# Dilated attention: three row loads at the start, a product moved ahead of the first scores, two score banks, and another layout for the queries in DRAM

## The reference, cut to what matters

```python
x = x + jnp.tanh(g_xattn[1]) * _L1_xattn_ref(_layernorm(x, axis=-1), ctx_1024, ctx_1024, ...)
# _L1_xattn_ref: q = x Wq + bq, k and v from the context, 16 heads of 16; per branch (segment, dilation):
scores = jnp.einsum("bqhd,bkhd->bhqk", qd, kd) * D ** (-0.5)
scores = jnp.where(mask, scores, -jnp.inf)
lse = jax.nn.logsumexp(scores, axis=-1)
o = jnp.einsum("bhqk,bkhd->bqhd", jnp.exp(scores - lse[..., None]), vd)
```

## Time and profile before

| | us |
|---|---|
| median of 3 runs | 838.92 (836.3 to 841.04) |
| the profiled execution, its own time | 843.52 |
| its span, first to last instruction | 841.8 |
| PE busy in the span | 638.2 (76%) |
| DVE busy | 503.8 (60%) |
| ACT busy | 429.2 (51%) |
| POOL busy | 352.3 (42%) |
| mean granted clock of PE, of full speed | 0.866 |

### The profile page before, as it was taken

How to read it: one execution, slowest core, us unless ns; L and a number is a source line. 1 busy time by engine, 2 the same in 40 slices (tenths; PEclk the granted TensorE clock), 3 DMA queues, 4 the chain that set the end, 5 groups by cost and what they waited for, 6 DMA issues and landing times. The chain is left out here.

```text
span 841.8 us, 14246 instructions
## 1 busy us (share of the span) xinstructions
PE 638.2 (76%) x4856; PEld 477.8 (57%) x4856; DVE 503.8 (60%) x1627; ACT 429.2 (51%) x815; POOL 352.3 (42%) x482
## 2 busy tenths in 40 slices
PE   3989899649999999999524778877987732138995
PEld 2878778427778778877412445544544521026774
DVE  0466655866666666664115577778775617857741
ACT  1353532218766876677111466556755616417753
POOL 2133325273563365353312443444533316534644
PEclk9998999859999999999855798889988955559998
DMA  6244214263553465342311222223210015503433
GB/s 194 69 124 140 85 51 143 97 190 91 137 152 95 104 142 151 93 87 32 49 52 32 59 77 63 81 57 97 81 39 28 26 38 189 194 26 73 85 52 38
DMA packets 73881, 76.07 MB, mean 90 GB/s; under 512 B 8037, under 2 KB 66449, under 8 KB 73553
## 3 DMA queue, kind: packets, MB, share of 16 engines
q1 hardware_dynamic: 61217, 59.32, 22.2%
q0 software_dynamic: 10928, 15.57, 11.0%
q10 hardware_dynamic: 1664, 0.27, 0.2%
HBM read 52.20 MB, written 22.94 MB: 89 GB/s over the span
## 5 line engine op out<-in xcount | busy, mean ns | idle before, releaser
L1876 DVE CUSTOM_DVE_ANT_0 c_sn<-c_ps_s,k_mask 128x128 f32<-128x128 f32 (+1 forms) x256 | 75.8, 352 | 55.3 <-PE c_ps_s L2014 55.3
L1708 POOL TENSOR_SCALAR_AFFINE_SELECT c_pr<-c_pr 128x512 f32<-128x512 f32 x64 | 42.9, 671 | 108.9 <-ACT c_pr L1767 107.8
L1398 PE MATMUL b_ps_y<-e_w2h,b_hh 128*128 128x256 f16 x320 | 87.3, 273 | 1.4 <-DVE b_yb L1312 0.6
L1398 PE MATMUL b_ps_y<-e_w2l,b_hh 128*128 128x256 f16 x320 | 87.2, 273 | 0.0
L1398 PE MATMUL b_ps_y<-e_w2h,b_hl 128*128 128x256 f16 x320 | 87.2, 273 | 0.0
L1281 DVE TENSOR_TENSOR b_hl<-b_h,b_hh 128x640 f16<-128x640 f32 x64 | 53.2, 832 | 47.5 <-ACT b_hh L1229 47.5
L1207 POOL DMA_INDIRECT res<-b_y,b_s_idx x40 | 65.2, 1631 | 37.7 <-ACT b_y L1246 27.4
L1193 POOL DMA_INDIRECT e_xg<-rows,e_g_idx x35 | 38.6, 1104 | 81.8 <-DVE e_g_idx L1322 71.2
L2042 PE MATMUL c_ps_v<-c_pr,k_vx 128*64 128x256 f32 (+1 forms) x512 | 62.1, 368 | 5.6 <-POOL c_pr L1708 4.8
L1767 ACT ACTIVATE c_pr<-c_ps_t 128x768 f32<-128x768 f32 x64 | 51.7, 808 | 13.2 <-PE c_ps_t L2028 13.2
L1361 PE MATMUL b_ps_h<-b_xh,e_w1h 128*128 128x320 f16 x256 | 56.7, 303 | 1.0 <-DVE b_xl L1286 0.9
(11 more groups left out here) (421 smaller groups left out, 1817.3 us busy)
## 6 DMA issues: line engine op xcount, KB each, us to landing
e_w<-in_L_ffn_W_dram SPq DMA_DIRECT2D x16, 1024.0 KB, 6.0
d_raw<-in_L_ffn_W_down_dram SPq DMA_DIRECT2D x8, 640.0 KB
k_ks<-kT SPq DMA_DIRECT2D x48, 64.0 KB, 2.6
c_qs<-q SPq DMA_DIRECT2D x48, 64.0 KB, 2.4
d_raw<-in_L_ffn_W_up_dram SPq DMA_DIRECT2D x4, 682.0 KB, 4.0
rows<-a_rows SPq DMA_DIRECT2D x8, 264.0 KB, 2.5
rows<-c_rows SPq DMA_DIRECT2D x8, 264.0 KB, 2.2
a_x_in<-in_x_dram SPq DMA_DIRECT2D x8, 256.0 KB, 3.0
```

What stands on the lines that cost most here:

```text
L1398: last = pe.matmul(ps_y[(j + CT) % 2][:, 0:D], a, b[:, f, :], start=(f == 0 and k == 0), stop=(f == FC - 1 and k == 2))
L1708: pool.affine_select(out=late, in_=late, compare_op=ALU.is_ge, fill=0.0, base=0, pattern=[[0, 2], [0, 2], [1, P]], channel_multiplier=-1). ...
L1876: dve.tensor_tensor_reduce(sn[r][:, a:b], ps_s[:, r, a:b], mask[:, a:b], -1.0, 3.0e38, ALU.add, ALU.min, mx[g % 2][:, q, r, j:j + 1]).then ...
```

## The change

What it does, part by part:

- `load_x(0)`, `load_x(1)` and `load_x(2)` are issued together at the start of the stage; the later loads keep their places.
- For batch 1 the turn of xn and the query product (`rows_turn`, `queries`) stand at place 0 of step -2, before batch 0's first score tile, in place of 6 and 7; DVE's `stats` of batch 1 moves to place 0 of that step, behind ql of batch 0.
- Batch 0's score tiles alternate between ps_s and ps_t, each waits for the maxima of the last but one, and sn has four buffers.
- For batch 0 the turn of the maxima stands ahead of batch 1's first score tile, and its first by_keys (with its exp) one place earlier.
- For all batches the queries' way through DRAM is another: `dram["q"]` holds 32 rows of 8 pairs by 256. Each half is stored as soon as it is there, in two DMAs, one for each c; two loads bring the high half into 32 rows each (the same 16 rows twice, a repeat of 2 in front of the source), two more the low half into 16 rows each. There are semaphores for the high and the low store apart.

```diff
-        sn = some(2, "sn", [P, QK])
+        sn = some(4, "sn", [P, QK])
...
+        def first_scores_in_t(g, j):
+            return g == 0 and j % 2 == 1
...
-            load_x(0)
+            for first in range(3):
+                load_x(first)
...
                 if within(f):
-                    landed(sp, s_ldq, f, 2, 96)
+                    landed(sp, s_ldq, f, 2, 64)
                     apart(sp, s_passs)
-                    after(sp, s_qh, f)
-                    after(sp, s_ql, f)
-                    for part, src in enumerate((qh, ql)):
-                        sp.dma_start(dram["q"][f % 2, part].rearrange("(c p) t -> p c t", p=P), src[f % 2][:])\
-                            .then_inc(s_qst[f % 2], 16)
-                    landed(sp, s_qst, f, 0, 32)
+                    for done_, stored, part, src in ((s_qh, s_qsh, 0, qh), (s_ql, s_qsl, 1, ql)):
+                        after(sp, done_, f)
+                        for c in range(C):
+                            sp.dma_start(dram["q"][f % 2, part, :, 4 * c:4 * c + 4, :].rearrange("k b t -> b k t"),
+                                         src[f % 2][:, c, :]).then_inc(stored[f % 2], 16)
+                    landed(sp, s_qsh, f, 0, 32)
                     done(sp, s_pt, (f - 2) * HH)
-                    for part, which in enumerate((0, 0, 1)):
-                        for r in range(2):
-                            a = 64 * r + HD * part
-                            sp.dma_start(qs[f % 3][a:a + HD, :, :], by_head(dram["q"][f % 2, which], HD)[r])\
-                                .then_inc(s_ldq[f % 3], 16)
+                    for r in range(2):
+                        sp.dma_start(qs[f % 3][64 * r:64 * r + 2 * HD, :, :],
+                                     dram["q"][f % 2, 0, r * HD:(r + 1) * HD, :, :].unsqueeze(0)
+                                     .to_broadcast([2, HD, HH, T]))\
+                            .then_inc(s_ldq[f % 3], 16)
+                    landed(sp, s_qsl, f, 0, 32)
+                    for r in range(2):
+                        a = 64 * r + 2 * HD
+                        sp.dma_start(qs[f % 3][a:a + HD, :, :], dram["q"][f % 2, 1, r * HD:(r + 1) * HD, :, :])\
+                            .then_inc(s_ldq[f % 3], 16)
...
-                if within(e + 1):
+                if within(e + 1) and e + 1 >= 3:
                     load_x(e + 1)
...
-                    if p + 1 == HH and within(g):
+                    if p + (2 if g == 0 else 1) == HH and within(g):
                         exps(g, 0)
...
+                bank = ps_t if first_scores_in_t(g, j) else ps_s
...
-                        dve.tensor_tensor_reduce(sn[r][:, a:b], ps_s[:, r, a:b], mask[:, a:b], -1.0, 3.0e38,
+                        dve.tensor_tensor_reduce(sn[2 * (j % 2) + r][:, a:b], bank[:, r, a:b], mask[:, a:b], -1.0, 3.0e38,
...
-                    if p == 4 and within(e):
+                    if p == (0 if e == 1 else 4) and within(e):
                         landed(dve, s_ldx, e)
...
-                done(pe, s_mx, (g * HH + j) * 4)
+                done(pe, s_mx, (j - 1 if g == 0 else g * HH + j) * 4)
+                bank = ps_t if first_scores_in_t(g, j) else ps_s
...
+                    if p == 0 and e == 1:
+                        rows_turn(e)
+                        queries(e)
...
-                    if p + 1 == HH and within(g):
+                    if p + (2 if g == 0 else 1) == HH and within(g):
                         by_keys(g, 0)
                     if p < 4 and within(g):
                         scores(g, p + 4)
+                    if p == 4 and g == 0:
+                        maxima_turn(n, g)
                     if p >= 4 and within(f):
                         scores(f, p - 4)
...
+                    if p == 4 and within(g) and g > 0:
+                        maxima_turn(n, g)
...
-                    if p == 6 and within(e):
...
+                    if p == 6 and within(e) and e != 1:
+                        rows_turn(e)
+                    if p == 7 and within(e) and e != 1:
+                        queries(e)
...
-        "q": nc.dram_tensor("q", [2, 2, S.D, S.T], F16).ap(),
+        "q": nc.dram_tensor("q", [2, 2, 2 * S.HD, S.H // 2, S.T], F16).ap(),
```

More of the change, by code:

```diff
@@ L1572, in attention_dilated @@
         s_ldm = [sem("ldm0"), sem("ldm1"), sem("ldm2")]
-        s_qst = [sem("qst0"), sem("qst1")]; s_mst = [sem("mst0"), sem("mst1")]
+        s_qsh = [sem("qsh0"), sem("qsh1")]; s_qsl = [sem("qsl0"), sem("qsl1")]
+        s_mst = [sem("mst0"), sem("mst1")]
         s_st = sem("st"); s_mv = sem("mv"); s_var = sem("var"); s_rstd = sem("rstd"); s_mr = sem("mr")
@@ L1687, in _ @@
             for u in range(2):
-                for pair, per in ((s_qst, 32), (s_mst, 16), (s_xst, 16), (s_rst, 16)):
+                for pair, per in ((s_qsh, 32), (s_qsl, 32), (s_mst, 16), (s_xst, 16), (s_rst, 16)):
                     sp.wait_ge(pair[u], per * B // 2)
@@ L1842, in step @@
                         after(act, s_qf, e)
-                        landed(act, s_qst, e, 2, 32)
+                        landed(act, s_qsh, e, 2, 32)
                         act.activation(qh[e % 2][:], qf[:], ACT.Copy).then_inc(s_qh, 1)
@@ L1903, in step @@
                         after(dve, s_qh, f)
-                        landed(dve, s_qst, f, 2, 32)
+                        landed(dve, s_qsl, f, 2, 32)
                         dve.tensor_tensor(ql[f % 2][:], qf[:], qh[f % 2][:], ALU.subtract).then_inc(s_ql, 1)
@@ L2013, in scores @@
                         a = 64 * r
-                        last = pe.matmul(ps_s[:, r, lo:hi], q[a:a + 3 * HD, j, rows_], key[a:a + 3 * HD, j, 0:keys],
+                        last = pe.matmul(bank[:, r, lo:hi], q[a:a + 3 * HD, j, rows_], key[a:a + 3 * HD, j, 0:keys],
                                          start=True, stop=True)
@@ L2055, in turned, with maxima_turn, rows_turn, queries @@
                 last.then_inc(s_ot, 1)
+            def maxima_turn(n, g):
+                after(pe, s_mlo, g)
+                done(pe, s_av, n * HH + 4)
+                for q in range(2):
+                    last = pe.matmul(ps_v[0:4 * HH, T + (1 - q) * P:T + (2 - q) * P],
+                                     mhl[g % 2][:, q, :, :, :].rearrange("p r l b -> p (r l b)"), ident_h[:],
+                                     start=True, stop=True)
+                last.then_inc(s_pm, 1)
+            def rows_turn(e):
+                after(pe, s_xn, e, 0, 2)
+                after(pe, s_oT, e, 4)
+                if e:
+                    after(pe, s_xT, e - 1)
+                turn(ps_a, xn[e % 2], swap=True).then_inc(s_pxt, 1)
+            def queries(e):
+                after(pe, s_xT, e)
+                after(pe, s_x3, e, 4, 2)
+                if e:
+                    after(pe, s_qf, e - 1)
+                product(ps_b, wT[:, 0], xT).then_inc(s_pq, 1)
             over_tensor(pe)
@@ L2067, in step @@
                         scores(g, p + 4)
+                    if p == 4 and g == 0:
+                        maxima_turn(n, g)
                     if p >= 4 and within(f):
                         scores(f, p - 4)
-                    if p == 4 and within(g):
-                        after(pe, s_mlo, g)
-                        done(pe, s_av, n * HH + p)
-                        for q in range(2):
-                            last = pe.matmul(ps_v[0:4 * HH, T + (1 - q) * P:T + (2 - q) * P],
-                                             mhl[g % 2][:, q, :, :, :].rearrange("p r l b -> p (r l b)"), ident_h[:],
-                                             start=True, stop=True)
-                        last.then_inc(s_pm, 1)
+                    if p == 4 and within(g) and g > 0:
+                        maxima_turn(n, g)
                     if within(n):
@@ L2107, in step @@
                         product(ps_b, oT, wT[:, 1]).then_inc(s_po, 1)
-                    if p == 6 and within(e):
-                        after(pe, s_xn, e, 0, 2)
-                        after(pe, s_oT, e, 4)
-                        turn(ps_a, xn[e % 2], swap=True).then_inc(s_pxt, 1)
-                    if p == 7 and within(e):
-                        after(pe, s_xT, e)
-                        after(pe, s_x3, e, 4, 2)
-                        product(ps_b, wT[:, 0], xT).then_inc(s_pq, 1)
+                    if p == 6 and within(e) and e != 1:
+                        rows_turn(e)
+                    if p == 7 and within(e) and e != 1:
+                        queries(e)
             for n in range(-3, B + 2):
```

2 lines of the change are left out of this document (1 added, 1 removed).

## The result

The changed kernel took 851.15 us (median of 4 runs, 850.62 to 852.04) against 839.98 for the kernel before on the same chip: a ratio on record of 1.011 with a 95% interval of 1.0069 to 1.0152 (the two medians alone would make it 1.013). The forecast was 839.1 with a range up to 844.0. The time went the way of the third rival (847.7: the two-engine loads set the loop), and the sign that the prediction named for it, a wait for q before every batch, is there.

A forecast was written before the change was run, and what follows sets the result against it. VectorE and TensorE set the loop's length; the start is a filling pipeline with waits for queries. Batch 2's scores 0.15 us earlier plus 0.3 for a colder start gave about +0.2 on 838.92: 839.1, range 833.0 to 844.0.

The forecast's parts named there:

- the third rival: Dilated attention loop: at 0.22 us a 4 KB packet, two-engine high loads delay every batch, 8.8 us slower, 847.7; chance 0.12.
- Shape sets the number of engines: Queries' DRAM transfers: the smaller leading count decides, so new stores run on 4 engines, high loads on 2, low loads on 16.
- Both loads on the same pair, 0.16 us a packet: High-half query loads: both use the same two engines, 32 packets of 4 KB on each, at 0.161 us a packet.
- Stores on four engines: Query stores to DRAM: 512-byte packets at 0.0274 us on 4 engines, 1.75 us for two stores, 3.5 for all four.
- 10.33 us from qh to the scores: Queries through DRAM, from qh's end to first scores: 0.96 + 3.5 + 5.15 + 0.32 + 0.4 us; before, 7.69.
- 32 x 0.161 = 5.15: Time in us of the two high loads: 32 packets of 4 KB on each of two shared engines.
- The margin: Loop, batches 3 to 7: the queries' way could take 1.35 us more than its forecast 10.33 us without cost.
- the point of 11.68 us: Loop: length of the way from qh to the scores up to which it costs nothing; 0.20 us a 4 KB packet.
- Batch 0 behind the second product: Start of dilated attention: batch 0's scores wait for batch 1's product, ending 443.65, 2.68 us later; q(0) lands by 443.61.
- Two banks, 1.12 us a head; ql(1) 4 us earlier: Batch 0's heads run at VectorE's pace, 1.12 us each, so batch 1's low query half ends 4.02 us earlier.
- The reordering loses nothing else: Start of dilated attention: four sn buffers cost nothing; the third x load was taken as 0 for x(0), at most 1.8 us.
- 0.3 for a colder start: Batch 2's scores: 0.3 us added because TensorE waits 4 us for q in place of 1.77.

## Why the prediction was wrong, point by point

- **Shape sets the number of engines**: right, from the closers: 4 a store and 2 a high load came, on 4.4 and 2.03 engines by the share. The runs with four loads (16 closers a load) and with high and low in one (2) show it too.
- **Both loads on the same pair, 0.16 us a packet**: right (2.03 engines; 24 packets of 4 KB in 2 us, and two chains in the packet records).
- **Stores on four engines**: right (16 closers), 0.0273 us a packet (forecast 0.0274).
- **10.33 us from qh to the scores**: wrong, and the step that failed: 12.27 in batch 0, 12.04 to 12.89 in the loop. The term mis-sized is "32 x 0.161 = 5.15" and the 0.32 behind it: 5.47 taken, 6.98 measured in batch 0 and 6.5 to 7.4 in the others. It counted packets at the price of a long quiet run and let both engines start at once. In batch 0 one engine starts 1.38 us late, behind an instruction fetch. In the loop both start within 0.5 us of each other, but their first packets take up to 1.1 us, and the value rows and the low loads pass beside them. Another 0.3 to 0.7 us came ahead of the loads, where 4.46 had been taken.
- **The margin**: the point of 11.68 us was right (11.75 by the ring). With only 1.35 us of margin, and under it a load that no row had shown at work, the third rival deserved more than its 0.12. That rival's way was 12.3 us and its places were nearly these (forecast 23.5, measured 23.44 for batch 0; 8.8 us in all, measured 9.2 by the ratio). Its reason, every packet dearer at 0.22, was not the one: most packets still took 0.16, so the near hit of its sum is partly luck.
- **Batch 0 behind the second product**: right but for q: the product ends 21.39 after the layer norm (forecast 21.53), then TensorE waits 2.04 for q. With a quick q it is 21.33.
- **Two banks, 1.12 us a head; ql(1) 4 us earlier**: right (1.11; 4.25 earlier with the old way of q, 2.3 in the changed kernel, whose scores began late).
- **The reordering loses nothing else**: right; 0.994 alone. The third row load costs nothing, as taken.
- **0.3 for a colder start**: it came (batch 2's first score tile takes 0.50 us at 483.03, at a granted clock of 0.50, where the kernel before has 0.34 at 1.00), but beside a wait of 5.78 us for q it has no weight.

So the gain of the reordering, 5 us, was there. The new way of q, put in to make it larger, took 14 us: part at the start, part in each turn of the loop.

## What to carry to other kernels

Merging two loads of 16 rows into one of 32 by a leading repeat of 2 saves a DMA and gave up 14 of 16 engines here (2 closers a load in place of 16); look at the leading count of both sides, and read it from the closing packets. Where two engines carry a load, its packets stand in two chains, and the load is done with the later one: in batch 0 that was the chain which began 1.38 us late, and it ended 0.51 us after the other. Don't price such a load from a long run on all engines. And where a stall has a slack in a loop, work out the ring (here 15.3 us from scores to qh, and the way back) before trusting a margin of one microsecond.

## What the runs showed of the hardware

- The DMAs followed here leave one packet of 4 bytes (0.009 us) for each engine that carries them. With two: in the changed kernel's batch 0 each of the two chains has one at the end of each high load, and the share there is 2.03 engines. With four: 16 for four stores led by 4, at 4.4 engines. With sixteen: 32 for two stores led by 128, at 14.6 engines, in the kernel before.
- Some of the first packets of a load on two engines are long. In the changed kernel's dilated attention the trace's packet records hold 16 packets of 4 KB that took 0.6 to 1.1 us, out of 800, all within 1.8 us of the first packet of a batch's high loads; the median of all is 0.16. With four loads of 16 rows the longest of the 800 took 0.52. Why was not settled.
- An instruction fetch seems to have held one of the two engines. In batch 0 it ran from 434.00 to 435.39, and the second chain's first packet starts at 435.39, as close behind it as one packet of a chain behind the other. That it sat on that engine is read from these times, since the records don't name engines.
- Beside a long fetch the row loads come late as well. In the three traces where a fetch of 0.87 to 1.14 us falls beside the first row loads, batch 0's layer norm starts 3.96 to 4.13 us after their issue; in the nine where the fetch there takes 0.31 to 0.42, it starts after 3.51 to 3.71. Which of the two delays the other, the traces don't say.
